# One decoder layer: batch 0 runs ahead through factors and projections, and experts' outputs are scattered to the tokens' rows

## What is computed

```
h   = layernorm(x)
q   = rope(h @ Wq)                       # per head
kv  = h @ Wkv ; kh, vh = split(h @ Wkvh) # one key and value per token, two factors per head
g   = h @ Wg
kv_head = cumsum((h @ Wkvh) * exp(cumsum of log_sigmoid(g), shifted by one))
k = rope(kp * kh) ; v = vp * vh          # factor per token and head
x = x + layernorm(softmax(causal(q k^T / sqrt(128))) v @ Wout)
h2 = layernorm(x)
top 2 of 8 experts per token; each expert takes at most 640 tokens, in order
routed = sum of weight * expert(h2) ; expert: silu(gate) * up, down
x = x + layernorm(routed + shared_mlp(h2))
```

## Time and profile before

| what | value |
|---|---|
| three runs | 839.72, 846.82 (median), 848.85 us |
| the profiled execution | 842.17 us |
| its span, first to last instruction | 840.4 us |
| busy: PE, DVE, POOL, ACT | 760.9, 614.5, 553.7, 490.4 us |
| mean granted clock of PE | 0.958 |

### The profile page before, as it was taken

The page is one execution under the profiler, slowest core; times in us unless marked ns, Lnnn a source line. Parts: engine busy times, 40 slices in busy tenths (PEclk is TensorE's granted clock), DMA queues, the critical chain, the costliest instruction groups (busy, mean ns, idle before and its releaser), DMA issues.

```text
span 840.4 us, 13976 instructions
## 1 busy us (share of the span) xinstructions
PE 760.9 (91%) x4344; PEld 634.0 (75%) x4344; DVE 614.5 (73%) x1561; ACT 490.4 (58%) x1155; POOL 553.7 (66%) x460
## 2 busy tenths in 40 slices
PE   3867999999999999999999999998992989999875
PEld 3755787888888888888888888887781888887543
DVE  6637999887988977888877889886731177774337
ACT  2638677777767767666776677675520355542332
POOL 1347878898788987788987888871065534325751
PEclk9969999999999999999999999999995999999965
DMA  9121224441221222212221212210421345522321
GB/s 305 50 88 58 69 83 151 136 136 64 64 76 62 66 70 63 72 64 64 77 64 64 76 63 64 72 43 26 128 82 72 110 144 186 186 76 94 100 88 51
DMA packets 47701, 75.74 MB, mean 90 GB/s; under 512 B 9680, under 2 KB 24592, under 8 KB 47632
## 3 DMA queue, kind: packets, MB, share of 16 engines
q1 hardware_dynamic: 43744, 65.46, 24.3%
q0 software_dynamic: 3072, 8.39, 3.1%
q10 hardware_dynamic: 816, 1.05, 0.4%
HBM read 57.71 MB, written 17.17 MB: 89 GB/s over the span
## 4 chain that ended last, share of the span: by engine, by line
PE 75%; DVE 9%; ACT 5%; issue 5%; another core or an unknown queue 3%; POOL 2%; DMA 1%; DVEq 0%; ACTq 0%; POOLq 0%
PE ps L377 19%; PE ps L869 17%; PE ps L837 14%; PE ps L885 11%; PE ps L855 8%; PE ps L980 5%; DVE xn L1116 1%; DVE hid_both L1468 1%; DMA x_sb<-in_x_dram 1%; DVE hid_hi L1458 1%; DVE hid L1463 1%; DVE hid L1455 1%; DVE s_hid L1396 1%; ACT y_sb L750 1%
## 5 line engine op out<-in xcount | busy, mean ns | idle before, releaser
L589 ACT ACTIVATE prob<-ps,neg_max 128x512 f32<-128x512 f32 (+3 forms) x256 | 132.6, 526 | 86.2 <-DVE neg_max L1184 86.2
L869 PE MATMUL ps<-pt,vp 128*128 128x512 f32 (+3 forms) x512 | 150.7, 437 | 4.6 <-issue 3.1
L869 PEld LDWEIGHTS ps<-pt,vp 128*128 128x128 f32 x512 | 83.2, 192 | 54.6 <-issue 19.1
L1569 POOL TENSOR_TENSOR q_lo<-q_sw,q_hi 128x512 fp32r<-128x512 f32 x64 | 85.9, 1342 | 47.9 <-ACT q_hi L611 47.9
L1184 DVE CUSTOM_DVE_ANT_0 ps<-ps,causal_row 128x512 f32<-128x512 f32 (+3 forms) x256 | 117.4, 520 | 0.0
L1579 POOL TENSOR_TENSOR o_lo<-o_t,o_hi 128x512 fp32r<-128x512 f32 x64 | 83.3, 1301 | 47.3 <-ACT o_hi L617 46.8
L837 PE MATMUL ps<-k_hi,q_hi 128*128 128x512 f32 (+3 forms) x256 | 91.0, 355 | 7.3 <-POOL q_lo L1569 5.0
L855 PE MATMUL ps<-id_f,prob 128*128 128x128 f32 x640 | 92.3, 275 | 2.4 <-ACT pt L598 2.4
L1203 DVE TENSOR_TENSOR k_lo<-kh_row,k_hi 128x512 fp32r<-128x512 f32 x64 | 83.4, 1303 | 8.1 <-ACT k_hi L605 8.1
L1560 POOL TENSOR_TENSOR q_sw<-q_sw,rope_sb 128x512 f32<-128x512 f32 x64 | 83.7, 1307 | 8.7 <-ACT q_sw L578 8.7
L1565 POOL TENSOR_TENSOR q_sw<-q_cos,q_sw 128x512 f32<-128x512 f32 x64 | 81.5, 1274 | 9.2
(11 more groups left out here) (199 smaller groups left out, 1962.5 us busy)
## 6 DMA issues: line engine op xcount, KB each, us to landing
kh_row<-kvh_rows SPq DMA_DIRECT2D x64, 256.0 KB, 3.2
inv_row<-inverse_sums SPq DMA_DIRECT2D x64, 256.0 KB, 3.1
slot_inputs<-zeros SPq DMA_DIRECT2D x8, 640.0 KB, 4.8
xg<-slot_inputs SPq DMA_DIRECT2D x8, 640.0 KB, 4.6
slot_outputs<-yo SPq DMA_DIRECT2D x8, 640.0 KB, 3.3
up_raw<-in_w_up_dram SPq DMA_DIRECT2D x8, 368.0 KB, 4.8
x_sb<-in_x_dram SPq DMA_DIRECT2D x4, 512.0 KB, 9.1
wo_raw<-in_wout_dram SPq DMA_DIRECT2D x4, 512.0 KB, 8.0
```

Source lines behind the costliest of these rows:

```text
L589: ins = act.activation(prob[:, i % 2, ROW_AT[nt]:ROW_AT[nt] + w], ps_s[bank][:, at:at + w], ACT.Exp, scale=-1.0, bias=neg_max[:, i % 2, nt ...
L869: ins = pe.matmul(ps_qo[:, mt * P:SEQ], vp[:, b * TPB + mt, :], pt[:, i % 2, cols], start=(mt == 0), stop=(mt == PT_BANKS[-1][-1]))
L1569: pool.tensor_tensor(q_lo[:, i % 2, :], q_sw[:], q_hi[:, i % 2, :].bitcast(F32), ALU.subtract) \
```

## The change

The front is reordered, and the way back from the experts is replaced.

- **Front.** x's first half batch is loaded by SP, the other half by ACT's queue; heads 0 to 3 of Wq before the cosines. The split of `w0` moves: cast on ACT, subtraction on POOL only after batch 0 is normalised. Batches 1 to 3 are normalised by ACT, with POOL taking the inverse root. Batch 0 goes alone through gates, keys, values and factors; `keys`, `gates` and `values` get banks of their own, and those of batches 1 to 3 lie between the queries and scores of units 0 to 3.
- **Factors.** Sigmoid becomes an Exp on ACT (in the copy out of PSUM) and, on DVE, a sum with 1 and a reciprocal. It is done twice: for batch 0's 32 rows in the front, and for all 128 rows in the steps of units 0 to 3 on DVE; the second store, turn and copy (`factors_as_columns(1)`) come at units 4 and 5. The rotated keys are summed on POOL instead of DVE.
- **Units 0 and 1** make their scores in one plain float32 pass, with no splits of queries and keys.
- **`rest_of_wq`** of heads 8 to 15 moves from DVE to the end of POOL's part of a unit. The shared weights' first load moves on SP from the front to unit 5.
- **Way back.** A slot's row carries two more columns: the slot of the token's first choice, and the token's number (rows of 258 floats). For each expert DVE works out the row of each slot's output (`rows_of_slots`), and POOL scatters the outputs by 5 indirect DMAs per expert (`scatter_rows`) to `yt_dram`, which has the first choices of all tokens and then the second ones, and is filled with zeros at units 12 to 19. `yo` has two buffers. At the end SP reads `yt_dram` by 16 plain DMAs of two tiles each, in order of tokens; `yg_dram`, its stores and the 32 gathers go. POOL now splits an expert's up weights one expert ahead, between `rest_of_down` and `scatter_rows`.

The diff, cut to its core:

```diff
@@ sync
-            sp.dma_start(x_sb[:, 0:TPB, :], x_v[0]).then_inc(x_in[0], 16)
+            sp.dma_start(x_sb[:, 0:2, :], x_v[0, :, 0:2, :]).then_inc(x_in[0], 16)
...
-            sp.dma_start(kvh_dram, hc_t).then_inc(kvh_stored, 16)
+            sp.dma_start(kvh_dram[0:2 * H, :], hc_t[0:2 * H, :]).then_inc(kvh_stored, 16)
...
             for i in range(UNITS):
+                if i == FACTOR_STEP - 1:
+                    sp.wait_ge(hc_ready, 2)
+                    sp.dma_start(kvh_dram[2 * H:, :], hc_t[2 * H:, :]).then_inc(kvh_stored, 16)
+                if i == FACTOR_STEP:
+                    sp.wait_ge(kvh_stored, 32)
+                    load_shared(0)
...
@@ sync, experts and end
-                        sp.wait_ge(xg_psum, 3 * e + 3)
+                        sp.wait_ge(rows_ready, e + 1)
                         load_slots(e + 2, r)
...
-                    sp.wait_ge(yo_ready, 3 * e + 6)
-                    sp.dma_start(yg_dram[bass.ds(e * CAP, CAP), :].rearrange("(p s) e -> p s e", p=P), yo) \
-                        .then_inc(yo_stored, 16)
...
+            sp.wait_ge(yo_stored, NE * 16 * ST)
+            for g in range(TILES):
+                t, k = g // 2 * 2, g % 2
+                if g >= GR:
+                    sp.wait_ge(got_used, 2 * (g - GR) + 2)
+                rows = yt_dram[k * T + t * P:k * T + (t + 2) * P, :]
+                sp.dma_start(got[:, g % GR, :, :], rows.rearrange("(t p) e -> p t e", p=P)).then_inc(got_in[g % GR], 16)
@@ scalar
+            std_of_first()
+            act.wait_ge(w0_in, 16)
+            act.copy(w0_hi[:], w0_raw[:]).then_inc(w0_hi_ready, 1)
+            head_of_wq(0, WCH)
+            head_of(0)
+            normalize_x(1)
+            gates_of(0)
+            swapped_keys(0)
+            head_of(1)
+            values_of(0)
+            normalize_x(2)
             swap_q(0)
...
+            gates_of(1)
+            swapped_keys(1)
+            values_of(1)
+            head_of(2)
             swap_q(1)
+            factors_as_columns(0)
+            normalize_x(3)
+            head_of_wq(WCH, 2 * WCH)
+            swap_q(2)
+            gates_of(2)
             exps(0)
+            swapped_keys(2)
+            head_of(3)
+            values_of(2)
             head_of_keys(2)
             head_of_queries(2)
+            gates_of(3)
+            swapped_keys(3)
+            values_of(3)
             exps(1)
@@ scalar, unit i
+                if i == FACTOR_STEP:
+                    factors_as_columns(1)
@@ scalar, expert
-                    act.wait_ge(yo_stored, 16 * e + 16)
+                    act.wait_ge(yo_free, e + 1)
@@ tensor
+            turn_x(0)
+            gates(0)
+            keys(0)
+            values(0)
+            turn_x(1)
             queries(0)
...
+            gates(1)
+            keys(1)
+            values(1)
             queries(1)
+            turn_x(2)
+            turn_factors(0)
+            pe.wait_ge(k_cos_ready, 1)
             pe.wait_ge(vcol_ready, 1)
             scores(0)
             queries(2)
+            gates(2)
+            keys(2)
+            values(2)
+            turn_x(3)
             scores(1)
+            gates(3)
+            keys(3)
             queries(3)
+            values(3)
@@ vector
+            def sigmoids(k):
+                n = 2 * H * B if k else 2 * H
+                dve.wait_ge(gate_copied, B if k else 1)
+                done(dve.tensor_scalar(f_t[0:n, :], f_t[0:n, :], 1.0, None, ALU.add))
+                done(dve.reciprocal(f_t[0:n, :], f_t[0:n, :]))
...
+                if i == 0:
+                    sigmoids(1)
+                if i == 1:
+                    products_of_gates(1)
+                if i == 2:
+                    scaled_gates(1)
+                if i == 3:
+                    sums_of_gates(1)
...
+            def rows_of_slots(e, r):
+                dve.wait_ge(xg_in[r], 8 * (e - r) + 16)
+                dve.wait_ge(yo_free, e + 1)
+                dve.tensor_tensor(is_first[:], xg[:, r, :, E], slot_no[:], ALU.is_equal).then_inc(row_steps, 1)
+                dve.wait_ge(row_steps, 2 * e + 1)
+                dve.tensor_scalar(slot_no[:], slot_no[:], float(CAP), None, ALU.add)
+                dve.scalar_tensor_tensor(row_of[:], is_first[:], -float(T), xg[:, r, :, E + 1], ALU.mult, ALU.add) \
+                    .then_inc(row_steps, 1)
+                dve.wait_ge(row_steps, 2 * e + 2)
+                dve.tensor_scalar(to_row[:, r, :], row_of[:], SKIP, None, ALU.add).then_inc(rows_ready, 1)
@@ gpsimd
+                if i and wq_head(i - 1) is not None:
+                    rest_of_wq(wq_head(i - 1), wq_head(i - 1) + 1)
...
+            def scatter_rows(e, r):
+                if e:
+                    pool.wait_ge(yo_stored, 16 * ST * e)
+                    pool.sem_inc(yo_free, 1)
+                pool.wait_ge(rows_ready, e + 1)
+                for k, (t0, n) in enumerate(YO_BANKS):
+                    pool.wait_ge(yo_ready, 3 * e + 3 + k + 1)
+                    for t in range(t0, t0 + n):
+                        pool.indirect_dma_start(
+                            yt_dram[:, :], bass.IndirectOffsetOnAxis(ap=to_row[:, r, t:t + 1], axis=0), yo[:, r, t, :],
+                            None, bounds_check=2 * T - 1, oob_is_err=False).then_inc(yo_stored, 16)
...
+            split_up(0, 0, True)
+            split_up(1, 1, True)
+            for e in range(NE):
+                rest_of_down(e, e % 2)
+                if 1 <= e < NE - 1:
+                    split_up(e + 1, (e + 1) % 2, False)
+                scatter_rows(e, e % 2)
```

More of the change, by code:

```diff
@@ L81, in decoder_layer @@
     BIG = 3e38
+    EW = E + 2
     SQ = 32
@@ L241, in decoder_layer @@
         iota_sb = small("iota_sb", [NE])
+        below, token_no, slot_no = small("below", [1]), small("token_no", [TILES]), small("slot_no", [ST])
+        token_steps, slot_steps = small("token_steps", [NE]), small("slot_steps", [ST])
+        is_first, row_of = (small(n, [ST]) for n in ("is_first", "row_of"))
+        to_row = small("to_row", [2, ST], U32)
         group_w = [TPB * (B - 1), TPB]
@@ new lines, in scaled_gates, with sums_of_gates @@
+            def scaled_gates(k):
+                n = 2 * H * B if k else 2 * H
+                done(dve.tensor_tensor(kvh_t[0:n, :], kvh_t[0:n, :] if k else ps[GATE_BANK[0]][0:n, :], fcum_t[0:n, :], ALU.mult))
+            def sums_of_gates(k):
+                n = 2 * H * B if k else 2 * H
+                if k:
+                    dve.wait_ge(vcol_ready, 1)
+                    dve.wait_ge(kvh_stored, 16)
+                dve.tensor_tensor_scan(hc_t[0:n, :], ones_t[0:n, :], kvh_t[0:n, :], 0.0, ALU.mult, ALU.add).then_inc(hc_ready, 1)
@@ L1278, in rest_of_turned, with numbers @@
                                       ALU.subtract).then_inc(xt2_lo, 1)
+            def numbers():
+                done(dve.tensor_reduce(below[:], before_b[:], AX.X, ALU.add))
+                dve.scalar_tensor_tensor(token_steps[:], iota_sb[:], float(P), below[:].to_broadcast([P, NE]),
+                                         ALU.mult, ALU.subtract)
+                done(dve.scalar_tensor_tensor(slot_steps[:], below[:].to_broadcast([P, ST]), -float(ST), iota_sb[:, 0:ST],
+                                              ALU.mult, ALU.add))
+                for t in range(0, TILES, NE):
+                    dve.tensor_scalar(token_no[:, t:t + NE], token_steps[:], float(t * P + T - 1) - SKIP, None, ALU.add)
+                done(dve.tensor_scalar(slot_no[:], slot_steps[:], -float(ST), None, ALU.add))
             def split_shared(n):
@@ L1285, in split_shared, with first_scaled_keys @@
                 dve.tensor_tensor(sw_lo, sw_raw[n], sw_hi.bitcast(F32), ALU.subtract).then_inc(sw_split, 1)
+            def first_scaled_keys(i):
+                dve.wait_ge(kh_row_in[i], 16)
+                dve.wait_ge(kt_ready, 1)
+                dve.tensor_tensor(kh[:, i, :], kt[:, tok(0)], kh_row[:, i, :], ALU.mult).then_inc(kh_ready, 1)
+            stats_of_x(0)
+            normalize_first()
+            stats_of_x(1)
+            rest_of(0)
+            stats_of_x(2)
+            sigmoids(0)
+            products_of_gates(0)
+            dve.wait_ge(rope_in, 32)
+            cos_of_keys(0)
+            scaled_gates(0)
+            sums_of_gates(0)
+            rest_of(1)
+            cos_q(0)
+            stats_of_x(3)
+            cos_of_keys(1)
+            first_scaled_keys(0)
+            cos_q(1)
+            first_scaled_keys(1)
+            rest_of(2)
             dve.wait_ge(consts_made, 1)
-            cos_q(0)
-            rest_of_keys(0)
-            cos_q(1)
-            rest_of_keys(1)
             maxima(0)
             cos_q(2)
+            cos_of_keys(2)
+            rest_of(3)
+            inverses(0)
             rest_of_keys(2)
-            inverses(0)
             maxima(1)
+            cos_of_keys(3)
             dve.wait_ge(vcol_ready, 1)
@@ L1316, in _ @@
                         scale_x2(b)
```

(12 more changed lines are left out.)

383 lines of the change are left out of this document (171 added, 212 removed).

## The result

The changed kernel takes 837.59 us (median of 20 runs, 835.77 to 841.18), the kernel before 843.31 us (20 runs, 839.72 to 848.85): a ratio of 0.9929, 95% interval 0.9914 to 0.9943. The spans of the two profiled executions, 840.4 and 835.6 us, differ by 4.8 us, which can be split by stage.

What follows compares the result with a forecast made beforehand. PE was taken to bound units 9 to 59, DVE units 0 to 8. From 842.2 us, front and units -12, experts +5 and end -19.5 gave 815.7, stated as 817 with part of the runs' higher median; range 802 to 836.

Steps and rivals of the forecast that it cites:

- the part on the experts: Experts' stage: 40 scatters at 1.29 us fill POOL's queue to 81.4 of 84.3 us; +5 us, from 0 to +12.
- The front: Before unit 0: factors ready sooner, first scores at 37.1 and first weighing of values at 65.3, a gain of 12.6 us.
- the rows' slope: Front, DVE's reciprocal of 512 columns: 6 ns a column from traced 4- and 16-column reciprocals, so 3.3 us.
- The estimate of 4.3 us: Front, DVE's reciprocal: the skill's repeat count of 8 at 0.96 GHz gives 4.3 us instead of 3.3.
- Units 0 to 8: First nine units, bound by DVE: 76.5 us instead of 77.2, a gain of 0.7, bounds -4 and +5.5.
- Step (5): Units 0 to 8: DVE loses `rest_of_wq`, 1.25 us in eight units; POOL gains it at some 0.7.
- The end: Stage after the experts: without gathers PE works on unstopped and the 16 reads are hidden; -19.5 us.
- standstill: Routing and end: PE nearly stops while POOL issues scatters or gathers, 0.03 us of work from 631.4 to 647.6; cause unknown.
- Rival A: Experts: the standstill goes with the scatters into the loop, +20 us there, kernel 837 us; chance 0.2.
- Rival C: Experts: DVE's instructions hold each scatter, POOL becomes the bound; a pitch of 2.15 us eats all other gains; chance 0.06.
- Rival B: Front gives a third, as ACT's list or a low clock holds PE: -4 us instead of -12, kernel 825; chance 0.14.
- The start of the sum: Whole kernel: 842.2 us, the profiled execution, with part kept of the 4.6 us by which the runs' median stood above it.

Runs made afterwards that it cites:

- e9: Changed kernel with the up weights split two experts ahead, as before the change, and without the experts' 40 scatters; 819.16 us in a single run.
- e3: Changed kernel without the experts' 40 scatters, POOL raising their semaphores itself, the new split order kept; 834.33 us in a single run.
- e6: e1 with the rest of the down weights moved from POOL to DVE, behind the first half's hidden units; 826.55 us, ratio to before 0.9812.
- e12: e8 with the rest of the next expert's down weights put between an expert's third and fourth scatter on POOL; 816.73 us, ratio to before 0.9675.
- e5: Changed kernel, split still one expert ahead but waiting until DVE has finished the current expert's hidden units; 825.14 us, ratio to before 0.9789.
- e1: Changed kernel with POOL splitting the up weights two experts ahead again, scatters and all else kept; 827.99 us, ratio to before 0.9817.
- e4: Changed kernel with the subtraction on Wq of eight heads moved back from POOL to DVE; 842.81 us, ratio to before 0.9993.
- e7: e1 with POOL waiting for landing after every fourth of the routing's 32 scatters; 829.4 us, ratio to before 0.9836.
- e8: e1 with POOL waiting for landing after every eighth of the routing's 32 scatters; 824.64 us, ratio to before 0.9758.
- e10: e6 with POOL waiting for landing after the first and second group of an expert's scatters; 845.73 us, ratio to before 1.0052.

## Why the prediction was wrong

**The step that failed** is the part on the experts: "I take +5, from 0 (POOL fits) to +12." It measured +19.8, and that is 14.8 of the 21.7 us between the forecast's sum of 815.7 and the profiled execution's 837.4; 5.1 more lie ahead of the experts and 1.8 in the end. The step counted `split_up` of the next expert among POOL's 11.0 us per expert, at its new place, and asked only whether the queue fits. It did not ask what that place is beside: the diff moves the split from two ahead to one ahead, and the wait that kept it behind DVE's work becomes empty. That part costs 15.4 us (e9 to e3), 8.2 of it waits of PE and 7.2 its lower clock, for which the step had no term, and is none of the three rivals. POOL itself, forecast above 90% busy, worked 64.55 of 104.10 us. The share of the scatters, 3.0 in this order and 6.7 in the old one, was inside the forecast's 0 to 12, in part by luck: the forecast's reason was POOL's queue, and the runs show ACT's lag in its place (e6, e12). With the moment or the order put back and the scatters kept, the kernel takes 825.14 us (e5) or 827.99 (e1), both inside the range.

Three things would have shown it. An instruction of DVE was known to take longer beside POOL's (an `xn` of 3.15 us beside POOL's subtraction against 1.38). The order was in the diff. And the Trainium skill (SBUF — State Buffer, Who interferes with whom) says that GpSimd and VectorE share a pair of ports, that a VectorE instruction with two SBUF inputs, or a cast in its two-port mode, contends with GpSimd, and that whoever is second is blocked for the whole instruction. The trace agrees: 0.33 to 1.52 us and 0.49 to 1.97, ending 0.18 and 0.35 us after POOL's instructions.

**The front was right.** First gates 13.46 (forecast 13.4), reciprocal 3.34 us (3.3 by the rows' slope), last scan done at 25.83 (25.4), first scores 38.88 (37.1), first weighing 66.61 (65.3): a gain of 11.3 us instead of 12.6. In the profiled executions of the runs that share this front, the first weighing lies between 66.48 and 69.48. The estimate of 4.3 us from the Trainium skill (VectorE: DVE Perf Modes, First, the fixed hardware budget) was too long here.

**Units 0 to 8** took 78.30 us instead of the forecast's 76.5. The miss is unit 0, with 10.50 us instead of 8.4; units 1 to 3 took 25.9 (forecast 26.1) and 4 to 8 took 42.0 (42.0 with the 1.5 at unit 5). Its weighing comes after pauses of PE of 1.98 and 2.69 us and takes 4.60 us instead of 2.32, at a granted clock of 0.52 from 67 to 72 us; the forecast had 1 us for that. These are the weighing and the window of unit 0:

```profile
66.61 4.60 PE L912 MATMUL ps<-pt,vp 128*128 128x512 f32 x8 [2.69 <-issue]
```

```profile
66.61:77.11 10.50, 9.21 (x36) 6.25 (x37) 8.67 (x20) 6.36 (x16) 6.95 (x5) 0.75 0.13 41
```

Step (5)'s trade of DVE's time for POOL's was worth 5 us (e4), as its sign said. `numbers()` was "one us of DVE at unit 15, where DVE has 1.2 us per unit free", at nothing. It took some 3.6 us of DVE and cost 1.56 us of PE (a pause before the weighing at 194.88): three of its instructions on 8, 8 and 5 columns took 1.13, 1.15 and 1.25 us, beside POOL, where another on 5 columns took 0.15.

```profile
190.43 1.13 DVE L1325 SCALAR_TENSOR_TENSOR token_steps<-iota_sb,below 128x8 f32<-128x8 f32 x1
191.48 0.15 DVE L1327 SCALAR_TENSOR_TENSOR slot_steps<-below,iota_sb 128x5 f32<-128x5 f32 x1
```

All in all -6.9 until the experts' start, within the bounds of -18 to -4: 11.3 won at the first weighing, 1.1 lost in units 0 to 8, 1.2 from there to the last unit's weighing, and 2.1 from that to the experts' first product. The last 2.1 had no term in the forecast, and no run asks for their cause.

**The end was right**: -17.7 for -19.5, PE 40.00 of 40.00 us busy from 780 to 820, no standstill, the reads hidden. (The terms given there add up to 820.7, not 820.9.)

**Rival A** has the number, 837 with +20 for the experts, by luck: of the measured +19.8 the scatters cost 3.0. It was wrong in its place and mechanism, and right in kind: scatters in a row do delay other engines in the loop, by up to 1.7 us an expert at the old order (e1, e6), not by a standstill. In the changed kernel the lag is 0.04 us but in one expert (0.62 and 0.54): when PE's last product ends there, POOL is at `rest_of_down`. **Rival C**: the scatters kept 1.02 us on average (median 0.97, the longest of 40 1.98), far from a mean pitch of 2.15. The factor of five that the Trainium skill (SBUF — State Buffer, A bandwidth-pool intuition that's wrong (but worth ruling out)) has for a DMA beside a copy on DVE does not show. **Rival B** is refuted by the first weighing. The start of the sum was right: 842.2 and the 1.3 kept of the three runs' median make 843.5, and 20 runs gave 843.31.

**Open**: why a row of scatters holds signals or engines. That pauses end the standstill (e7, e8), and that the lag goes without the scatters (e9) and with other work in between (e12), is shown; through what the row acts, and whether its length or its moment decides, is not.

## What to carry to other kernels

When a diff reorders a queue, price not only how long each piece takes but which wait it now meets, whether that wait still holds anything back, and what runs on the neighbouring engine at the new moment. A wait can be the thing that keeps two engines apart: e5 only raised the value that one waits for and gained 12 us. A long row of indirect DMAs is better broken up than issued in one go: in the loop other work of the same queue did it (e12) where waits for landing cost more than they gave (e10), and in the routing a wait after every eighth brought the experts' start forward by 6.2 us (e8).

## What the runs showed of the hardware

Beside a row of 24 scatters, 1.29 us apart, ACT waited 9.66 and 14.91 us and PE worked 0.33 us of 14.60; a wait for landing after every fourth or eighth, 2.3 to 2.5 us each, removed it. A row of five gave a lag of up to 1.7 us to ACT's Silu after PE's product; with two subtractions of 0.7 to 1.0 us after the third, the lag was 0.04 us in seven experts of eight. Three tiny DVE instructions (8, 8 and 5 columns) took 1.13, 1.15 and 1.25 us beside POOL's of some 1.3, instead of 0.15. The experts' stage pays for PE's waits twice: with the order of the changed kernel the same 558 products took 86.07 us at clock 0.90 instead of 77.19 at 1.00; in e1, with 14.5 us of waits instead of 18.0, the clock stayed at 1.00.
